# A fused adapter, normalisation and top-2 expert layer: the order of its opening work and its last transposes

## The reference, cut to what matters

```
# layer 0, an adapter chosen by the sample's first id
hidden = gelu(x @ down_W.T + down_b)                       # 32 wide
hidden = expert[id](hidden) + domain_emb[id]
x1 = layernorm(hidden @ up_W.T + up_b + x) * g0 + b0

# layer 1
h = layernorm(x1) * ln_g + ln_b                            # over features
h = (h - mean over tokens) / sqrt(var over tokens)         # per sample and feature
sty = small MLP of subj_emb[second id]                     # 64 -> 128 -> 128 -> 64 -> 256
h = h * (softplus(sty[:128]) + 1e-8) + sty[128:]
gates = top 2 of softmax(h @ router_w), renormalised       # 8 experts
y = sum over experts e of gates[e] * (relu(h @ w1[e] + b1[e]) @ w2[e] + b2[e])
return x1 + y
```

## Time and profile before

| | |
|---|---|
| median of 3 runs | 119.65 us |
| profiled execution | 119.94 us, of which 118.2 us span from first to last instruction |
| PE busy | 112.0 us (95% of the span), 519 matrix instructions |
| DVE busy | 91.8 us (78%) |
| ACT busy | 84.3 us (71%) |
| POOL busy | 54.1 us (46%) |
| granted PE clock | full in each of the 40 slices |
| chain that ended last | PE 72%, DVE 14%, ACT 5%, DMA 3% |

### The profile page before, as it was taken

One profiled execution on the slowest core, in us unless ns is written; L12 is line 12 of the kernel. 1 busy time (PEld: TensorE's weight loads), 2 busy tenths in 40 slices (PEclk: granted clock), 3 DMA queues, 4 the chain that ended last, 5 costly groups with the idle time before them and its releaser, 6 DMA issues.

```text
span 118.2 us, 1665 instructions
## 1 busy us (share of the span) xinstructions
PE 112.0 (95%) x519; PEld 84.3 (71%) x519; DVE 91.8 (78%) x228; ACT 84.3 (71%) x153; POOL 54.1 (46%) x75
## 2 busy tenths in 40 slices
PE   6799988999999999999999999999999999999990
PEld 2157534777777888688888888888888888888780
DVE  4486988999899989997685959595867777776772
ACT  2139845698999988697878787878778687878400
POOL 5020889226417000101259999976758941322310
PEclk9999999999999999999999999999999999999999
DMA  4939699994000000326999300000000000000005
GB/s 68 343 97 365 173 374 442 384 412 150 0 0 3 0 6 0 89 100 165 415 446 408 169 0 6 0 0 0 0 0 0 0 0 0 6 0 0 0 0 178
DMA packets 4473, 14.17 MB, mean 120 GB/s; under 512 B 561, under 2 KB 1905, under 8 KB 4209
## 3 DMA queue, kind: packets, MB, share of 16 engines
q1 hardware_dynamic: 3024, 9.67, 21.9%
q0 software_dynamic: 1008, 3.67, 8.8%
q10 hardware_dynamic: 432, 0.73, 2.2%
HBM read 13.52 MB, written 0.56 MB: 119 GB/s over the span
## 4 chain that ended last, share of the span: by engine, by line
PE 72%; DVE 14%; ACT 5%; issue 3%; DMA 3%; POOL 1%; DVEq 0%; ACTq 0%; POOLq 0%
PE bank L594 22%; PE bank L595 22%; PE bank L633 12%; PE bank L613 11%; DMA ids_i<-ids_dram 3%; DVE x L913 2%; ACT hid_high L508 2%; DVE stats L920 1%; ACT bank L511 1%; DVE hid_low L1005 1%; DVE bank L905 1%; POOL z L370 1%; PE bank L750 1%; DVE stats L876 1%; PE bank L583 1%
## 5 line engine op out<-in xcount | busy, mean ns | idle before, releaser
L508 ACT ACTIVATE hid_high<-bank,early_sb 128x512 fp32r<-128x512 f32 x64 | 44.2, 691 | 15.9 <-PE bank L613 15.8
L1005 DVE TENSOR_TENSOR hid_low<-bank,hid_high 128x512 fp32r<-128x512 f32 x51 | 34.8, 687 | 16.7 <-ACT bank L511 16.1
L511 ACT ACTIVATE bank<-bank,early_sb 128x512 f32<-128x512 f32 x51 | 33.6, 658 | 0.0
L308 POOL TENSOR_TENSOR w_low<-w_raw,w_high 128x256 fp32r<-128x256 f32 x32 | 22.7, 734 | 12.3 <-DMA w_high<-w_all_dram 4.4
L633 PE MATMUL bank<-hid_low,w_high 128*128 128x512 f32 x64 | 25.9, 405 | 0.4 <-DVE hid_low L1010 0.2
L594 PE MATMUL bank<-h_high,w_low 128*128 128x512 f32 x64 | 25.5, 398 | 0.3 <-ACT h_high L486 0.3
L594 PE MATMUL bank<-hid_high,w_low 128*128 128x512 f32 x64 | 25.6, 400 | 0.0
L595 PE MATMUL bank<-h_high,w_high 128*128 128x512 f32 x64 | 25.3, 396 | 0.0
L613 PE MATMUL bank<-h_low,w_high 128*128 128x512 f32 x64 | 25.1, 397 | 0.0
L595 PE MATMUL bank<-hid_high,w_high 128*128 128x512 f32 x64 | 25.0, 390 | 0.0
L318 POOL TENSOR_TENSOR y_sum<-y_sum,y_part 128x512 f32<-128x512 f32 x9 | 11.6, 1292 | 17.3 <-DVE y_part L1025 15.1
(11 more groups left out here) (136 smaller groups left out, 99.2 us busy)
## 6 DMA issues: line engine op xcount, KB each, us to landing
w_high<-w_all_dram POOLq DMA_DIRECT2D x7, 512.0 KB, 7.9
w_raw<-w_all_dram SPq DMA_DIRECT2D x1, 2560.0 KB, 10.9
gate_all<-gate_scratch SPq DMA_DIRECT2D x4, 512.0 KB, 5.9
gate_all<-gate_scratch SPq DMA_DIRECT2D x1, 2048.0 KB, 12.5
w_raw<-w_all_dram SPq DMA_DIRECT2D x3, 512.0 KB, 3.9
style_sb<-style_dram SPq DMA_DIRECT2D x1, 324.0 KB, 5.6
tables_sb<-tables_dram ACTq DMA_DIRECT2D x1, 272.0 KB, 3.8
xT_sb<-xT_dram SPq DMA_DIRECT2D x1, 256.0 KB, 4.4
```

Source lines behind the costliest of these rows:

```text
L308: nc.gpsimd.tensor_tensor(w_low[:, e % W_RING, quarter(q)], w_raw[:, e, quarter(q)], w_high[:, e % W_RING, quarter(q)].bitcast(F32), ALU.s ...
L508: ac(hid_high[:, slot, :], hid_ps[slot][:, :], ACT.Relu, bias=bias).then_inc(relu_steps, 1)
L511: ac(hid_ps[slot][:, :], hid_ps[slot][:, :], ACT.Relu, bias=bias).then_inc(relu_steps, 1)
L1005: v.tensor_tensor(low, ps, high.bitcast(F32), ALU.subtract).then_inc(low_vector, 1)
```

## The change

Seven edits, all in the order of work or in where it runs; the DMAs are the same.

- PE makes all four `down` products first (samples 2 and 3 wait for `x_loaded[1]`), and `residual(1)` after the product of the up weights (L654).
- `residual(1)` and the eight products with the identity at the end are now transposes (`is_transpose`), also where they add to what is in PSUM.
- The first three style steps run on ACT.
- The three last steps of the softplus run on POOL, between `normalise(0, T)` and `load_high(2)`, from a ReLU of gamma that ACT makes besides; DVE's `feature_affine` waits for them before L963.
- POOL makes only the first two low quarters of expert 0 ahead of `normalise`; the other two and all four of expert 1 come after `affine_ready`, ahead of `load_high(4)`.
- Tile 3 is normalised on DVE instead of ACT. ACT rounds the first expert's weights one quarter at a time between style steps.
- DVE's order is by sample: both `centre`, then sample 0 to its shift, then sample 1. PE's fill is split around the transposes of sample 0.

```diff
-WARM_LOAD, WARM_NORM = 9, (2, 2, 6, 6, 3, 2)
+WARM_LOAD, WARM_NORM = 9, (2, 2, 3, 2, 6, 3, 2)
@@ POOL
+            def softplus():
+                pool.wait_ge(gamma_relu_ready, 1)
+                pool.wait_ge(soft_ln, 1)
+                nc.gpsimd.tensor_tensor(gamma_T[:, :], gamma_relu[:, :], soft[:, 2, :], ALU.add).then_inc(gamma_steps, 1)
+                pool.wait_ge(gamma_steps, 1)
+                nc.gpsimd.tensor_scalar(gamma_T[:, :], gamma_T[:, :], 1e-8, None, ALU.add).then_inc(gamma_steps, 1)
+                pool.wait_ge(gamma_steps, 2)
+                nc.gpsimd.tensor_scalar(minus_gamma[:, :], gamma_T[:, :], -1.0, None, ALU.mult).then_inc(gamma_steps, 1)
+                nc.gpsimd.tensor_scalar(gamma_g[:, :], gamma_T[:, :], col(C_LNG), None, ALU.mult).then_inc(gamma_steps, 1)
             load_high(1)
-            split_lows(0)
+            split_lows(0, (0, 1))
             normalise(0, T)
-            split_lows(1, (0, 1))
+            softplus()
             load_high(2)
             load_high(3)
             pool.wait_ge(affine_ready, HB)
-            split_lows(1, (2, 3))
+            split_lows(0, (2, 3))
+            split_lows(1)
             load_high(4)
@@ ACT
+            act.wait_ge(style_in_psum, 1)
+            ac(se_T[:, :], se_ps, ACT.Copy).then_inc(style_ready, 1)
+            act.wait_ge(style_in_psum, 2)
+            ac(hyp1_T[:, :], hyp1_ps, ACT.Relu, bias=col(C_HB1)).then_inc(style_ready, 1)
             act.wait_ge(eps_ready, 1)
             token_root(0, tiles(0, 2))
-            round_first_weights((0, 1, 2))
+            round_first_weights((0,))
+            act.wait_ge(style_in_psum, 3)
+            ac(hyp2_T[:, :], hyp2_ps, ACT.Identity, bias=col(C_HB2)).then_inc(style_ready, 1)
+            round_first_weights((1,))
             act.wait_ge(style_in_psum, 4)
             ac(sty1_T[:, :], sty1_ps, ACT.Relu, bias=col(C_SB1, SC)).then_inc(style_ready, 1)
-            round_first_weights((3,))
+            round_first_weights((2,))
+            token_root(1, tiles(0))
             act.wait_ge(style_in_psum, 6)
             ac(gamma_raw[:, :], gam_ps, ACT.Identity, bias=col(C_SBG)).then_inc(gamma_beta_ready, 1)
+            ac(gamma_relu[:, :], gam_ps, ACT.Relu, bias=col(C_SBG)).then_inc(gamma_relu_ready, 1)
             ac(beta_T[:, :], bet_ps, ACT.Identity, bias=col(C_SBB)).then_inc(gamma_beta_ready, 1)
-            token_root(1, tiles(0))
+            token_root(1, tiles(1))
             soft_exponential()
-            token_root(1, tiles(1))
             soft_logarithm()
-            normalise(T + 1)
+            round_first_weights((3,))
@@ PE
             down(0)
             down(1)
-            residual(1)
+            down(2)
+            down(3)
             pe.wait_ge(w_diag_ready, 1)
...
-            down(2)
-            down(3)
+            residual(1, one_pass=True)
             pe.wait_ge(ones_ready, HB)
             pe.wait_ge(up_eff_ready, 1)
             up(0)
...
             warm(WARM_NORM[2], bank[3])
             transpose_z(0)
+            warm(WARM_NORM[3], bank[3])
             pe.wait_ge(soft_in, 1)
             transpose_z(1)
-            warm(WARM_NORM[3], bank[3])
+            warm(WARM_NORM[4], bank[3])
@@ PE, end (both groups of products)
-                       start=(t == 0), stop=False, skip_group_check=True)
+                       is_transpose=True, start=(t == 0), stop=False, skip_group_check=True)
...
-                              start=False, stop=True, skip_group_check=True)
+                              is_transpose=True, start=False, stop=True, skip_group_check=True)
@@ DVE
                 after(("f_mean", h))
+                ve.wait_ge(gamma_steps, 4)
...
             sum_stats(0)
             sum_stats(1)
-            style_step(0)
             token_mv(0, 0, HB)
-            style_step(1)
             ve.wait_ge(ln0_loaded, 16)
             centre(0)
-            style_step(2)
+            centre(1)
             adapter_out(0)
-            centre(1)
             x1_stats(0)
+            token_mv(1, 0)
             adapter_out(1)
-            token_mv(1, 0)
+            x1_shift(0)
             x1_stats(1)
+            token_mv(1, 1)
             minus_abs()
-            token_mv(1, 1)
-            x1_shift(0)
             normalise(1)
             x1_shift(1)
-            softplus(0)
-            softplus(1)
-            softplus(2)
+            normalise(T + 1)
             feature_stats(0)
```

More of the change, by code:

```diff
@@ L138, in adapter_moe @@
         gamma_raw = sb("gamma_raw", [P, B])
+        gamma_relu = sb("gamma_relu", [P, B])
         beta_T = sb("beta_T", [P, B])
@@ L215, in adapter_moe @@
         gamma_beta_ready = sem("gamma_beta_ready")
+        gamma_relu_ready, gamma_steps = sem("gamma_relu_ready"), sem("gamma_steps")
         soft_in, soft_exp, soft_ln = sem("soft_in"), sem("soft_exp"), sem("soft_ln")
@@ L474, in soft_logarithm @@
                 ac(soft[:, 2, :], soft[:, 1, :], ACT.Ln, bias=1.0).then_inc(soft_ln, 1)
[L476 to L479, removed]
             def round_h(h):
@@ L560, in down, with residual @@
                    start=True, stop=True, tile_position=(0, row)).then_inc(down_in_psum, 1)
-            def residual(b):
+            def residual(b, one_pass=False):
                 for t in range(T):
                     mm(sum_ps[b][:, t, :], xT_sb[:, (b * T + t) * P:(b * T + t + 1) * P], ident[:, :],
-                       start=(t == 0), stop=False, skip_group_check=True)
+                       is_transpose=one_pass, start=(t == 0), stop=False, skip_group_check=True)
             def up(b):
@@ L580, in transpose_z @@
                 if b != 2:
-                    pe.wait_ge(*((z_vector, 1), (z_scalar, 1), None, (z_vector, 2))[b])
+                    pe.wait_ge(z_vector, (1, 2, None, 3)[b])
                 for t in range(T):
@@ L821, in _ @@
                             ).then_inc(up_eff_ready, 1)
-            def style_step(k):
-                ve.wait_ge(style_in_psum, k + 1)
-                if k == 0:
-                    v.tensor_copy(se_T[:, :], se_ps).then_inc(style_ready, 1)
-                elif k == 1:
-                    v.tensor_scalar(hyp1_T[:, :], hyp1_ps, col(C_HB1), 0.0, ALU.add, ALU.max).then_inc(style_ready, 1)
-                else:
-                    v.tensor_scalar(hyp2_T[:, :], hyp2_ps, col(C_HB2), None, ALU.add).then_inc(style_ready, 1)
             def minus_abs():
@@ L837, in minus_abs @@
                                        ).then_inc(soft_in, 1)
-            def softplus(k):
-                if k == 0:
-                    ve.wait_ge(soft_ln, 1)
-                    v.scalar_tensor_tensor(gamma_T[:, :], gamma_raw[:, :], 0.0, soft[:, 2, :], ALU.max, ALU.add
-                                           ).then_inc(vec_steps, steps.add())
-                elif k == 1:
-                    after("softplus")
-                    v.tensor_scalar(gamma_T[:, :], gamma_T[:, :], 1e-8, None, ALU.add).then_inc(vec_steps, steps.add())
-                else:
-                    after("softplus")
-                    v.tensor_scalar(gamma_g[:, :], gamma_T[:, :], col(C_LNG), None, ALU.mult
-                                    ).then_inc(vec_steps, steps.add())
-                    v.tensor_scalar(minus_gamma[:, :], gamma_T[:, :], -1.0, None, ALU.mult
-                                    ).then_inc(vec_steps, steps.add())
-                mark["softplus"] = steps.n
             mark = {}
```

7 lines of the change are left out of this document (3 added, 4 removed).

## The result

| | before | after |
|---|---|---|
| median of 6 runs | 119.25 us (119.07 to 119.68) | 120.9 us (120.41 to 125.66) |
| ratio | | 1.0119, 95% interval 1.0089 to 1.0150 |
| profiled execution's span | 118.2 us | 119.0 us |
| PE busy, matrix instructions | 112.0 us, 519 | 110.9 us, 508 |

Two of the six executions after, 125.48 and 125.66, had a mean granted clock of about 0.945; the ratio leaves them out, and the profile after is of one at full clock.

A forecast was written before the change was run, and what follows sets the result against it. PE, 95% busy, was taken as the bound, leaving only the opening and the end to move. 119.94 - 0.02 (opening) - 0.24 (end) = 119.68, or 119.4 us against the median; own range 119.1 to 119.7, over all cases 118.75 to 120.2.

The forecast's parts named there:

- All down products first: Opening on PE: waiting for the second half of x moves `up` from 8.98 to 9.30, +0.33.
- POOL's held quarters between DVE's low parts: L989 and L994 on DVE while POOL has more quarters queued: DVE keeps its pair together, cost 0.
- POOL going between: Rival at L989 and L994: a POOL quarter goes between, first `first_low` 0.53 later, 119.9 us; chance 0.25.
- The end: One-pass transposes at L750 and L756: DVE's output steps end 0.45 sooner, SP's last issue gains, -0.24 (0.15 to 0.45).
- DVE by sample, style on ACT, softplus step unstretched: Opening, `up` to sample 1's variance: style -0.53, unstretched L836 -0.50, order by sample +0.33, +0.24 and +0.05.
- Tile 2 beside tile 3: POOL's tile 2 takes 0.51 instead of 0.45 with DVE's tile 3 beside it, +0.06.
- Softplus on POOL: POOL behind tile 2: steps done at 17.8, cost 0, upper end +0.5; the late rival had chance 0.07.
- Granted clock below full: Sign of wrong: PE has less fill around the transposes, so the clock could fall; no size given.

The follow-up runs named there:

- e2: Changed kernel, with POOL's four low quarters of expert 1 waiting until both low parts of h are made; ratio 1.0049 to the kernel before.
- e12: Kernel before with POOL's new order of low quarters, expert 1's waiting for both low parts of h; 119.0 us, ratio 0.9957.
- e10: e8 with the new tile gamma_relu allocated last, no instruction differing; ratio 0.9967 to the kernel before.
- e6: Kernel before with only the one-pass transposes at the end; ratio 0.9980.
- e18: e10 with the first three style steps back on DVE and without the extra PE fill; ratio 1.0001 to the kernel before.
- e15: Kernel before with only the first three style steps on ACT, in the change's order; ratio 1.0064.
- e16: The changed kernel run once more, unaltered; ratio 1.0098 to the kernel before.
- e5: Kernel before with only the four down products first, residual(1) behind the up weights; ratio 1.0049.
- e9: Kernel before with only POOL's held low quarters, softplus staying on DVE; ratio 1.0018.
- e8: e7 with ACT taking the first inverse root ahead of the second style step; ratio 1.0007 to the kernel before.
- e3: Changed kernel with down products of samples 2 and 3 back behind the up weights, plus the wait of e2; ratio 1.0118 to the kernel before.
- e7: e3 with four filling products in PE's wait for the first style copy; ratio 1.0041 to the kernel before.
- e1: Changed kernel with down products of samples 2 and 3 back behind the up weights, residual(1) ahead of them; ratio 1.0101 to the kernel before.

## Why the prediction was wrong

The sum said -0.26 in the profile's terms; the profiles gave +0.85, so 1.11 is missing: 0.51 at POOL's held quarters, 0.46 at the end (-0.24 predicted, +0.22 measured), 0.14 at `up` and at DVE's part of the opening. The medians missed by more, 120.9 against 119.4; most of the further 0.4 is that I moved the forecast down by 0.29 to the median of before, whose executions start earlier than the profiled one, while after the change the wait for x takes that earlier start away.

- **All down products first: mis-sized by its base.** The mechanism was right: L672 at 8.14 (predicted 8.12), `up` at 9.38 (9.30). x landed when it was assumed to. The size was right only against that one profile: +0.33 was worked out from `up` at 8.98, where the first half of x and the ids were late, and that profile stood 0.7 us above the median of six. I noted the distance to the median and left it. Against the 8.15 to 8.72 of the other profiles `up` at 9.38 is 0.7 to 1.2 late, and the edit alone costs 0.49% (0.6 us) in the medians.
- **POOL's held quarters between DVE's low parts: the step I chose wrongly.** I took 0 and gave the rival, POOL going between at +0.53, a chance of 0.25. It happened: L984 0.95, the stage 0.51 longer, and `e2` and `e12` take it away again. The price was worked out rightly from rows; only my reason for 0, that DVE starts its next instruction before its last one's end, was none: POOL's third quarter is recorded from 20.48, L984 from 20.72. The Trainium skill's rule in "SBUF — State Buffer", "Who interferes with whom", by which issue order decides, agrees with that.
- **The end: the step that failed in sign.** The instructions came as predicted: four each, DVE without a gap, SP's three issues in 1.48. But 5.11 became 5.33, where I had -0.24. The stores land later by 0.2 to 0.4: 0.2 because a new tile moved z by 32 bytes, and for the two last up to 0.2 more with the one-pass products. The diff shows the allocation; I took the landings as unchanged. Even with z in its old place the end gains only 0.06: the earlier issue is followed by a longer landing, 2.1 instead of 1.9 for the two last stores in `e10`.
- **DVE by sample, style on ACT, softplus step unstretched.** Predicted -0.41 from `up` to the variance, measured -0.34. The parts, by differences of single profiles: the unstretched step gives 0.36 (6.22 to 5.86 in `e12`), I had put it at 0.50, though the meeting with POOL's quarters depends on when the start falls (`e6`); the order costs 0.54 (`e18` against `e12`), I had 0.62; the rest, style on ACT with `up` late, gives about 0.52 (5.88 against 6.40), I had 0.53. What I missed is in ACT's list: the root behind the second style step is covered only while `up` is late (`e15`, 1.03 of waiting).
- **Tile 2 beside tile 3**: 0.52 (predicted 0.51), stage +0.04 (+0.06). Right.
- **Softplus on POOL**: ends at 17.44 + 0.29 = 17.73, predicted 17.8, and nothing waits. Right.
- **Granted clock below full**: named as a sign of wrong and left out of the numbers. It came in 2 of 12 executions of the change (the first series and `e16`).

Do the parts make the whole? `e10` is the change without down first, without the meeting of POOL and DVE and without the shifted tile: -0.33%. Adding `e5` (+0.49), `e9` against `e12` (+0.61) and `e8` against `e10` (+0.40) gives +1.17%, where +1.19% and, in `e16`, +0.98% were measured. The intervals of the terms are about 0.2 to 0.35 each, two of the differences are between series, and `e10` has the root and a fill moved as well, so the agreement is closer than the data earn. That the meeting costs is shown both ways, by adding and by removing it; that down first costs is shown by adding it (`e5`), while taking it out of the change gave nothing until the root was moved (`e3`, `e7`, `e8`); the shifted tile is shown in the landings of every profile. The proportion of the three is an estimate.

## What to carry to other kernels

Before costing an edit against a profiled execution that stands above the median, find out which of its landings were late: an edit that adds a wait on another transfer looks cheap in such an execution. When work is taken from one engine's early list to a later place, ask what will be queued there beside another engine's pair of two-input operations; one wait on the same semaphore that the reader uses took away the whole cost here (`e12` against `e9`, 0.6%, across two series). And where a new small tile would move a tile that DMAs store from, look at the landings; here it was enough to allocate it last.

## What the runs showed of the hardware

- **DVE and POOL take turns.** With one low quarter on POOL in its way DVE's subtraction took 0.65, with a further one started ahead of it 0.95, without 0.41 (`e12`); POOL's quarter behind such a subtraction took 0.91 instead of 0.73. Even a step on 4 columns took 0.57 beside POOL's quarters and 0.13 to 0.17 when it met none.
- **The place of a stored tile.** From byte 40992 instead of 40960 of each partition, a store of 256 KB took 2.4 us instead of 2.2, and one of 128 KB 2.3 instead of 2.0 to 2.1 (2.1 instead of 1.9 with the two-pass end), and the end 0.28 more (5.33 against 5.05). Two places only were tried; which property of the place it is stays open.
- **The granted clock can fall at a PE wait of about 1 us.** With 0.93 to 1.02 of waiting, ending near 10.7, it fell to 0.50 of full speed, the level of 1.2 GHz: in `e1` and `e15` from about 12 us on for some 7 us, in `e3` from between 10 and 11 us to between 20 and 21. Executions with a mean clock below 0.98 were 4 of 7 of `e1`, 5 of 6 of `e3` and 5 of 12 of `e15`; whether their executions at full clock had the same wait, no profile shows. With four products of zeros in that wait (`e7`, `e8`) all 24 were at 0.992 or more.
- **Landings stray from execution to execution.** In the profiles the ids (2.5 KB) landed 2.1 to 3.5 us after their issue, the first half of x 3.4 to 4.4 and the second 4.7 to 6.0.
